# A fused attention and feed-forward layer: the first 16 V units reordered, and the loads that feed them

## The chip, the cores and the metric

The kernel runs on one Trainium2 chip, on 8 cores at once. Each core handles one sequence of 4096 tokens, with no exchange between cores. Times are device microseconds of the slowest core. The granted TensorE clock of a stretch is given as a share of full speed, which is 2.4 GHz.

## The reference, cut to what matters

```python
normed = (x - mu) * rsqrt(var + 1e-5) * norm_g + norm_b       # x: [4096, 1024] per core
hv = silu(normed @ W_h + b_h); v, gate = hv[..., :2048], hv[..., 2048:]
qk = silu(normed @ W_qk + b_qk)                               # 128 wide
quad_q, lin_q, quad_k, lin_k = heads of (qk * gamma + beta)
attn = square(relu(quad_q @ quad_k^T / 256 + bias))           # groups of 256 tokens
lin_kv = lin_k^T @ v / n                                      # sum over all 4096 tokens
out = gate * (attn @ v + lin_q @ lin_kv)
x = layernorm(x + (out @ W_o + b_o + x))
x = layernorm(x + relu(x @ W1 + b1) @ W2 + b2)
```

Since `lin_kv` sums over all tokens, V of all tokens is computed before the gate and the output can start.

## The kernel before, in words

The work has three stages: first V and qk for all tokens, then per block of 512 tokens the gate, the attention and W_o, and last the feed-forward part. The change concerns the start of the first stage.

The tokens stand in 32 tiles of 128, four to a block. Wv (the V half of W_h) has four slices of 512 columns. A **unit** is one tile by one slice: 8 matmuls of 128x512. There are 128 of them. `unit(u)` (line 39) gives tile and slice of unit u: the first 32 go through tiles 0 to 7 with slice 0, then with slice 1, 2 and 3. After them each tile takes its four slices in a row.

Every engine walks through u in a loop of its own. An engine executes its instructions strictly in the order written, so the slots below set the order.

- A tile t below 8 comes from DRAM in f32. VectorE makes its statistics (`stats_a`), GpSimd computes the scale from them, and writes the normalized tile in bf16 (`norm0`, lines 560 to 569). TensorE transposes it at slot `t_slot(t)` (8 short matmuls, line 680). ScalarE and VectorE each evict a part of it into `nfm` (lines 891 and 976); from tile 3 on ScalarE takes 5 and VectorE 3 of the 8 columns.
- A unit's PSUM result gets its bias from VectorE (`v_bias`, line 1013, which waits for that slice of the bias `bv`) and its silu from ScalarE (line 901). Both stand at slot `bias_slot(w)` (line 50). Before the change units 0 to 7 get them at slots 5 to 7.
- The products for qk (`qk`, line 691) of blocks 0 and 1 stand at units 10 and 14. GpSimd makes the four heads of it (`head_lk`, `heads`, lines 575 to 584); TensorE transposes lin_k (`lk_transpose`, line 698) at units 13 and 17.
- `linkv_unit` (line 724) adds V of a unit to `lin_kv`, one matmul each, starting at unit 16 (`linkv_at`).
- Tiles from 8 on pass through three f32 buffers and are transposed by DMA (`columns`, line 391).

Transfers: SyncE issues x, the first slice of Wv in four pieces (`wvf`, cast to bf16 by ScalarE at line 884, at slot 0), the bias slices, Wqk, and stores of V. These go to the hardware queue q1. GpSimd issues slices 1 to 3 of Wv as casting transfers, in two halves each (line 550), to the software queue q0: slice 1 after `norm0(3)`, slices 2 and 3 after `norm0(7)`. The second wait of SyncE is for `s_n0` 6, which means that tiles 0 to 5 are normalized. Then it loads x of tiles 8 to 10.

Until x and the weights have come, TensorE runs 20 warm matmuls and 8 more after each of the first two transposes (line 670).

Of the kernel before, what the change touches and what calls it, by code (L numbers as in the profile page):

```python
# [20 lines left out]
NT = 32  # L21
# [14 lines left out]

def unit(u):
    if u < 32:  # L40
        return u % 8, u // 8
    return u // 4, u % 4
# [6 lines left out]

def bias_slot(u):  # L50

    return (5, 5, 6, 6, 6, 7, 7, 7)[u] if u < 8 else u


def linkv_at(u):

    if u < 16:
        return ()
    if u < 24:
        return (2 * u - 32, 2 * u - 31)  # L60
    return (u - LAG,)


def t_slot(t):

    if t < 8:
        return (0, 0, 0, 1, 3, 4, 5, 6)[t]
    if t < 12:
        return (16, 19, 22, 25)[t - 8]
    return 16 * (t // 4) - 22 + 4 * (t % 4)  # L70


def stat_slot(t):

    return (9, 12, 18)[t - 8] if t < 11 else t_slot(t - 1)


def aff_slot(b):
# [2 lines left out]


def qk_slot(b):
    return (10, 14)[b] if b < 2 else 16 * b


def lkt_slot(b):
    return (13, 17)[b] if b < 2 else 16 * b + 4


def pieces_before(t):
# [15 lines left out]
def build_program():  # L107
# [145 lines left out]
    def v_buffer(w):  # L253

        if w < 16:
            return vse[:, w * 512:(w + 1) * 512]
        i = ((w // 4 - 4) % 3) * 4 + w % 4
        return vst[:, i * 512:(i + 1) * 512]

# [4 lines left out]
    def wt(eng, s, v):  # L264
        if v > 0:
            eng.wait_ge(S[s] if isinstance(s, str) else s, v)
# [33 lines left out]
    def rs_chain(gp, k):  # L300
        add_eps(gp, k)
        power(gp, k)
# [41 lines left out]
    def emit_sync(sy):  # L344
        def load_x_first(t):
            sy.dma_start(out=x_tile(t), in_=x_h[t * 128:(t + 1) * 128, :]).then_inc(d_xs[t], 16)

        def load_bv(s):
            sy.dma_start(out=bv[:, s * 512:(s + 1) * 512],
                         in_=bv_h[:, s * 512:(s + 1) * 512]).then_inc(d_bv[s], 16)  # L350
# [14 lines left out]
        load_wv_first(2)  # L365
        load_wv_first(3)
        load_x_first(4)
        load_x_first(5)
        load_x_first(6)
        load_bv(0)  # L370
        load_x_first(7)
        load_bv(1)
        sy.dma_start(out=wqkf[:], in_=wqk_h[:, :]).then_inc(d_wqk, 16)
        load_bv(2)
        load_bv(3)

        def load_x(t):
            i, n = ring(t - 8, 3)
# [12 lines left out]
            sy.dma_start_transpose(out=dst, in_=n0_tile(t)).then_inc(d_T[t % 2], 16)  # L391

        def store_v(q):
            wt(sy, "s_vsi", 4 * q + 4)
            if q < 4:
                src, landed = vse[:, q * 2048:(q + 1) * 2048], d_vse
            else:
                i = (q - 4) % 3
                src, landed = vst[:, i * 2048:(i + 1) * 2048], d_vst[i]
            if q < 8:  # L400
                s, t0 = q // 2, (q % 2) * 4
                dst = bass.AP(v_sp.tensor, t0 * 128 * HID + s * 512, [[HID, 128], [128 * HID, 4], [1, 512]])
            else:
                dst = v_sp[q, :, :]
            sy.dma_start(out=dst, in_=src).then_inc(landed, 16)
# [8 lines left out]
        load_x(8)  # L414
        load_x(9)
        load_x(10)
        for u in range(0, NU + 6):
            for t in range(8, NT):
                if t_slot(t) == u:
                    columns(t)  # L420
                    if t + 3 < NT:
                        load_x(t + 3)
            if u == 12:
                sy.dma_start(out=biasT[:], in_=rel_h[:, :]).then_inc(d_rel, 16)
            if u >= 5 and (u - 5) % 4 == 0 and (u - 5) // 4 < NT:
                store_v((u - 5) // 4)
            for b in range(NB):
                if qk_slot(b) + 3 == u and b < 6:
                    store_h(b)
            if u == 119:  # L430

                for i in range(2):
                    wt(sy, d_T[i], 16 * 12)
                for t in range(4):
                    q = tok_tile(t)
                    sy.wait_ge(*v_stored(q))
                    sy.dma_start(out=vb[:, t * 2048:(t + 1) * 2048], in_=v_sp[q, :, :]).then_inc(d_v[t], 16)
# [107 lines left out]
    def emit_gpsimd(gp):  # L545
        gp.memset(mhalf[:], -0.5).then_inc(S["s_initp"], 1)

        def load_wv(s):
            for c in (0, 2048):
                gp.dma_start(out=wv[:, s * 4096 + c:s * 4096 + c + 2048],  # L550
                             in_=wv_h[s - 1, :, c:c + 2048]).then_inc(d_wv[s], 16)

        wt(gp, "s_initp", 1)

        def norm0(t):
            j = t % 8
            if t != 7:
                rs_chain(gp, t)
            x_landed(gp, t)
            shift(gp, t)  # L560
            if t == 6:
                add_eps(gp, t + 1)
            wt(gp, "s_nm", t + 1)
            if t >= 10:
                wt(gp, d_T[t % 2], 16 * ((t - 8) // 2))
            gp.tensor_scalar(n0_tile(t), x_tile(t), rstd[:, j:j + 1], nmr[:, j:j + 1],  # L566
                             ALU.mult, ALU.add).then_inc(S["s_n0"], 1)
            if t == 6:
                power(gp, t + 1)

        def head_lk(b):
            wt(gp, "s_qks", b + 1)
# [18 lines left out]

        for t in range(NT):
            norm0(t)
            if t == 3:
                load_wv(1)
            if t == 7:
                load_wv(2)
                load_wv(3)
            if t in (8, 9):
                head_lk(t - 8)  # L600
                heads(t - 8)
            if t % 4 == 1 and t >= 13:
                head_lk(t // 4 - 1)
                heads(t // 4 - 1)

            for k in range(pieces_before(t), pieces_before(t + 1)):
                j, c = k // 4, (k % 4) * 1024
                gp.dma_start(out=wg[:, j * 4096 + c:j * 4096 + c + 1024],
                             in_=wg_h[j, :, c:c + 1024]).then_inc(d_wg[j], 16)
# [55 lines left out]
    def emit_tensor(te):  # L665
# [17 lines left out]
        def qk(b):  # L683
            wt(te, "s_wcq", 1)

            wt(te, "s_nfa", 8)
            wt(te, "s_nfd", 8)
            wt(te, "s_aff", b - 1)
            for c in range(8):
                o_ = b * 4096 + c * 512  # L690
                mm = te.matmul(pb[7][:], wqk[:, c * 128:(c + 1) * 128], nfm[:, o_:o_ + 512],  # L691
                               start=(c == 0), stop=(c == 7))
            mm.then_inc(S["s_qk"], 1)

        def lk_transpose(b):
            wt(te, "s_lk", b + 1)
            for i in range(4):
                mm = te.transpose(pT[:, i * 128:(i + 1) * 128], lkfm[:, i * 128:(i + 1) * 128], ident)
            mm.then_inc(S["s_lkT"], 1)
# [177 lines left out]
    def emit_scalar(sc):  # L877
# [25 lines left out]
        for u in range(NU):  # L903
            for t in tiles_at(u):
                nfm_evict(t)
                for c in ((0, 1), (2, 3, 4, 5, 6, 7))[t] if t < 2 else ():
                    cast_wv(c)
            if u == 8:
                sc.wait_ge(d_wqk, 16)
                sc.copy(wqk[:], wqkf[:]).then_inc(S["s_wcq"], 1)  # L910
            if (b := block_at(qk_slot, u)) is not None:
                wt(sc, "s_qk", b + 1)
                wt(sc, "s_hd", b)
                sc.activation(qkf[:], pb[7][:], AF.Silu, bias=prm[:, P_BQK:P_BQK + 1]).then_inc(S["s_qks"], 1)
            for w in range(u + 1):
                if bias_slot(w) == u:
                    v_silu(w)
# [43 lines left out]
    def emit_vector(ve):  # L961
# [7 lines left out]
        def stats_a(t):  # L969
            x_landed(ve, t)  # L970
            bn_stats(ve, x_tile(t), t)
# [48 lines left out]
        for u in range(NU):  # L1020
            for t in tiles_at(u):
                nfm_evict(t)
                if t < 3:
                    stats_a(t + 2)
            if 1 <= u < 4:
                stats_a(u + 4)
            for t in range(8, NT):
                if stat_slot(t) == u:
                    stats_a(t)
            for b in range(2, NB):  # L1030
                if u in (aff_slot(b), aff_slot(b) + 1):
                    affine(b, u - aff_slot(b))
            if u == 40:
                ve.wait_ge(d_rel, 16)
                ve.tensor_scalar(biasT[:], biasT[:], float(QKD) ** 0.5, None, ALU.mult).then_inc(S["s_init"], 1)
            if (b := block_at(lkt_slot, u)) is not None:
                wt(ve, "s_lkT", b + 1)
                if b >= 2:

                    wt(ve, "s_lkv", max(w for w in range(NU) if unit(w)[0] // 4 == b - 2) + 1)  # L1040
                ve.tensor_copy(lktm[:, (b % 2) * 512:(b % 2 + 1) * 512], pT[:, 0:512]).then_inc(S["s_lkt"], 1)
            if u in (123, 126):
                attn((u - 123) // 3)
            for w in range(u + 1):
                if bias_slot(w) == u:
                    v_bias(w)
# [168 lines left out]
```

## Time and profile before

| what | value |
|---|---|
| median of 3 runs | 1713.78 us (1713.61 to 1718.76) |
| the profiled execution, its own time | 1716.85 us |
| its span on the slowest core (core 6) | 1715.3 us |
| spans of the other cores | 1709.4 to 1712.6 us |
| PE matmul, busy | 1694.6 us (99%), 8164 instructions |
| DVE / ACT / POOL busy | 549.6 / 409.3 / 289.5 us |

The page gives, for each engine, its busy time, and cuts the span into 40 slices. PE shows 9 tenths or more in all slices but the first (7) and the last (8). PE is the matmul engine, DVE VectorE, ACT ScalarE, POOL GpSimd, SP SyncE. The profiled execution's own time stands 1.55 us above its span.

### The profile page before, as it was taken

How to read it: one execution, taken by the hardware profiler on the slowest of the kernel's cores; microseconds unless marked ns; L12 is line 12 of the kernel's file. 1: busy time of each engine (PE TensorE's matmuls, PEld its weight loads, DVE VectorE, ACT ScalarE, POOL GpSimd, SP SyncE). 2: the span in 40 equal slices, each digit the busy share in tenths (PEclk: the TensorE clock that was granted, in tenths of full speed). 3: DMA queues.
4: the chain of work that ended last, by engine and by line, in shares of the span. 5: the costliest groups of instructions: out<-in, count | busy, mean ns of one | idle time of the engine just before them, and what ended most of it. 6: DMA issues, size and time to landing. Idle time of an engine off the chain costs nothing.

```text
span 1715.3 us, 23484 instructions; the slowest of 8 cores (1709.4 to 1715.3 us)
## 1 busy us (share of the span) xinstructions
PE 1694.6 (99%) x8164; PEld 795.0 (46%) x8164; DVE 549.6 (32%) x927; ACT 409.3 (24%) x602; POOL 289.5 (17%) x459
## 2 busy tenths in 40 slices
PE   7999999999999999999999999999999999999998
PEld 3444444544544545545444444444444444444443
DVE  6465553445445455454102021030110201202102
ACT  5233333221221322222320402203113031140220
POOL 5444421042232231331200000000000000000000
PEclk9999999999999999999999999999999999999999
DMA  9996757745746647635941022101121011200101
GB/s 255 215 215 165 199 141 173 184 122 158 162 135 167 145 142 178 153 125 119 254 131 48 39 50 74 25 37 62 38 86 26 37 62 38 86 1 25 74 3 47
DMA packets 119153, 188.51 MB, mean 110 GB/s; under 512 B 64768, under 2 KB 68992, under 8 KB 119040
## 3 DMA queue, kind: packets, MB, share of 16 engines
q1 hardware_dynamic: 104352, 158.69, 29.2%
q0 software_dynamic: 14688, 28.32, 11.9%
q8 instruction: 70, 1.15, 0.3%
q14 instruction: 43, 0.35, 0.1%
HBM read 139.53 MB, written 69.47 MB: 122 GB/s over the span
## 4 chain that ended last, share of the span: by engine, by line
PE 96%; DMA 2%; POOL 0%; issue 0%; DVE 0%; SPq 0%; POOLq 0%; DVEq 0%
PE pb L872 26%; PE pb L849 26%; PE pb L815 13%; PE pb L781 13%; PE pb L715 12%; PE pb L803 3%; PE pb L724 2%; PE pb L797 2%; DMA xt<-x 1%; DMA xs<-x 1%; PE pb L691 1%; PE pb L739 0%; DVE bnst L272 0%; POOL n0s L566 0%; SPq L354 0%
## 5 line engine op out<-in xcount | busy, mean ns | idle before, releaser
L849 PE MATMUL pb<-xfm,w1s 128*128 128x512 bf16 x2048 | 443.3, 379 | 0.0
L957 ACT ACTIVATE h<-pb,prms 128x512 bf16<-128x512 f32 x256 | 176.1, 688 | 652.9 <-PE pb L849 652.9
L849 PEld LDWEIGHTS pb<-xfm,w1s 128*128 128x128 bf16 x2048 | 200.4, 98 | 241.6
L1114 DVE TENSOR_TENSOR xr<-pb,xr 128x512 f32<-128x512 f32 x64 | 44.3, 692 | 700.1 <-PE pb L872 700.1
L715 PE MATMUL pb<-wvs,nfm 128*128 128x512 bf16 x1024 | 242.2, 380 | 1.3 <-DVE vtmp L1013 0.6
L781 PE MATMUL pb<-nfm,wgs 128*128 128x512 bf16 x1024 | 240.6, 379 | 0.0
L872 PE MATMUL pb<-w2a,h 128*128 128x512 bf16 x1024 | 231.5, 379 | 0.0
L815 PE MATMUL pb<-wos,gated 128*128 128x512 bf16 x1024 | 224.6, 379 | 0.0
L293 POOL TENSOR_SCALAR veps<-mv 128x1 f32<-128x1 f32 x96 | 21.6, 225 | 1044.9 <-DVE mv L283 1043.7
L872 PEld LDWEIGHTS pb<-w2a,h 128*128 128x128 bf16 x1024 | 100.2, 98 | 120.8
L715 PEld LDWEIGHTS pb<-wvs,nfm 128*128 128x128 bf16 x1024 | 99.7, 98 | 119.6 <-issue 3.6
L815 PEld LDWEIGHTS pb<-wos,gated 128*128 128x128 bf16 x1024 | 100.2, 98 | 116.1
L781 PEld LDWEIGHTS pb<-nfm,wgs 128*128 128x128 bf16 x1024 | 100.2, 98 | 97.2
L1053 DVE TENSOR_TENSOR gated<-pb,gate 128x512 bf16<-128x512 f32 x128 | 88.4, 691 | 169.9 <-PE pb L803 118.0
L927 ACT ACTIVATE gate<-pb,prms 128x512 f32<-128x512 f32 x128 | 88.0, 687 | 206.5 <-PE pb L781 206.5
L1013 DVE TENSOR_TENSOR vtmp<-pb,bvs 128x512 f32<-128x512 f32 x128 | 87.7, 690 | 104.3 <-PE pb L715 103.1
L872 PE MATMUL pb<-w2b,h 128*128 128x512 bf16 x512 | 121.0, 379 | 0.0
L872 PE MATMUL pb<-w2c,h 128*128 128x512 bf16 x512 | 120.9, 379 | 0.0
L901 ACT ACTIVATE vst<-vtmp 128x512 bf16<-128x512 f32 x112 | 70.5, 630 | 154.0 <-DVE vtmp L1013 154.0
L272 DVE BATCH_NORM_STATS2 bnst<-xr 128x6 f32<-128x512 f32 x128 | 85.6, 690 | 17.2 <-DVE xr L1114 11.3
L658 POOL TENSOR_TENSOR xr<-xr,b2s 128x1024 f32<-128x1024 f32 x32 | 75.4, 2355 | 88.9 <-ACT xr L934 88.9
L934 ACT ACTIVATE xr<-xr,nmr,rstd 128x1024 f32<-128x1024 f32 x32 | 39.6, 1237 | 194.7 <-DVE x2bf L1079 194.7
(62 smaller groups left out, 896.0 us busy)
## 6 DMA issues: line engine op xcount, KB each, us to landing
vb<-v_sp SPq DMA_DIRECT2D x32, 512.0 KB, 6.2
xr<-x SPq DMA_DIRECT2D x32, 512.0 KB, 12.9
x_sp<-xr SPq DMA_DIRECT2D x32, 512.0 KB, 2.6
xr<-x_sp SPq DMA_DIRECT2D x32, 512.0 KB, 6.3
out<-xr SPq DMA_DIRECT2D x31, 512.0 KB, 2.6
v_sp<-vst SPq DMA_DIRECT2D x28, 512.0 KB, 5.7
xt<-x SPq DMA_DIRECT2D x24, 512.0 KB, 6.3
w_sp<-w POOLq DMA_DIRECT2D x32, 256.0 KB, 13.0
```

The source lines that it names most:

```text
L272: ve.bn_stats(bnst[:, c:c + 6], src[:, 512 * h:512 * h + 512]).then_inc(S["s_bn"], 1)
L658: gp.tensor_tensor(xr[:, i * 1024:(i + 1) * 1024], xr[:, i * 1024:(i + 1) * 1024], b2[:], ALU.add).then_inc(S["s_x2b"], 1)
L715: mm = te.matmul(pb[v_bank(u)][:], nfm_tok(t, c), wv[:, s * 4096 + c * 512:s * 4096 + (c + 1) * 512], start=(c == 0), stop=(c == 7))
L781: mm = te.matmul(pb[4 + n % 2][:], wg[:, w_:w_ + 128], nfm[:, o_:o_ + 512], start=(c == 0), stop=(c == 7))
L815: mm = te.matmul(pb[2 + h][:], gated[:, k * 512 + i * 128:k * 512 + (i + 1) * 128], wo[:, h * 8192 + k * 512:h * 8192 + (k + 1) * 512], st ...
L849: mm = te.matmul(pb[4 + n % 2][:], w1[:, w_:w_ + 128], xfm[:, x_:x_ + 512], start=(c == 0), stop=(c == 7))
L872: mm = te.matmul(ps[:], h1[:, ci * 512 + i * 128:ci * 512 + (i + 1) * 128], w_, start=(ci == 0), stop=(ci == 31))
L901: sc.activation(v_buffer(w), vtmp[:, (w % 3) * 512:(w % 3 + 1) * 512], AF.Silu).then_inc(S["s_vsi"], 1)
L927: sc.activation(gate[:, (n % 3) * 512:(n % 3 + 1) * 512], pb[4 + n % 2][:], AF.Silu, bias=prm[:, P_BG + e:P_BG + e + 1]).then_inc(S["s_gsi ...
L957: sc.activation(h1[:, ci * 512:(ci + 1) * 512], pb[4 + n % 2][:], AF.Relu, bias=prm[:, P_B1 + ci:P_B1 + ci + 1]).then_inc(S["s_h1"], 1)
L1013: ve.tensor_tensor(vtmp[:, (w % 3) * 512:(w % 3 + 1) * 512], pb[v_bank(w)][:], bv[:, s * 512:(s + 1) * 512], ALU.add).then_inc(S["s_vad"], 1)
L1053: ve.tensor_tensor(gated[:, e * 512:(e + 1) * 512], pb[n % 2][:], gate[:, (n % 3) * 512:(n % 3 + 1) * 512], ALU.mult).then_inc(S["s_gat"], 1)
```

## The change

It reorders the first 16 units by a table: four tiles by two slices, then tiles 4 to 7 by the same two slices. It follows this with other slots for transposes, statistics, bias and silu, qk, lin_k and `linkv`. SyncE loads only bias slice 0 behind x 4, then waits until tiles 0 to 3 are normalized, and only then loads bias slice 1, x 5 to 7 and Wqk; bias slices 2 and 3 come behind x 10. GpSimd issues the two halves of slice 1 after `norm0(1)` and `norm0(2)`, those of slice 2 after `norm0(5)` and `norm0(6)`, and slice 3 after the heads of both first blocks, which both now stand behind `norm0(9)`.

```diff
+FIRST = ((0, 0), (1, 0), (2, 0), (3, 0), (0, 1), (1, 1), (4, 0), (2, 1),
+         (3, 1), (4, 1), (5, 0), (5, 1), (6, 0), (6, 1), (7, 0), (7, 1))
 def unit(u):
+    if u < 16:
+        return FIRST[u]
...
 def bias_slot(u):
-    return (5, 5, 6, 6, 6, 7, 7, 7)[u] if u < 8 else u
+    return (0, 2, 2, 4, 5, 5)[u] if u < 6 else u
 def linkv_at(u):
-    if u < 16:
+    if u < 18:
         return ()
+    if u < 22:
+        return (3 * u - 54, 3 * u - 53, 3 * u - 52)
...
-        return (0, 0, 0, 1, 3, 4, 5, 6)[t]                 # t_slot
+        return (0, 0, 0, 2, 4, 8, 10, 12)[t]
-    return (9, 12, 18)[t - 8] if t < 11 else t_slot(t - 1)   # stat_slot
+    return (4, 6, 7, 9, 11, 18)[t - 5] if t < 11 else t_slot(t - 1)
-    return (10, 14)[b] if b < 2 else 16 * b                 # qk_slot
+    return (13, 14)[b] if b < 2 else 16 * b
-    return (13, 17)[b] if b < 2 else 16 * b + 4             # lkt_slot
+    return (15, 17)[b] if b < 2 else 16 * b + 4
...
         load_x_first(4)
+        load_bv(0)
+
+        wt(sy, "s_n0", 4)
+        load_bv(1)
         load_x_first(5)
         load_x_first(6)
-        load_bv(0)
         load_x_first(7)
-        load_bv(1)
         sy.dma_start(out=wqkf[:], in_=wqk_h[:, :]).then_inc(d_wqk, 16)
-        load_bv(2)
-        load_bv(3)
...
         load_x(10)
+        load_bv(2)
+        load_bv(3)
...
-            if t != 7:
-                rs_chain(gp, t)
+            rs_chain(gp, t)
...
-            if t == 3:
-                load_wv(1)
-            if t == 7:
-                load_wv(2)
-                load_wv(3)
-            if t in (8, 9):
-                head_lk(t - 8)
-                heads(t - 8)
+            if t in (1, 2, 5, 6):
+                load_wv(1 + t // 4, 1 - t % 2)
+            if t == 9:
+                for b in range(2):
+                    head_lk(b)
+                    heads(b)
+                for half in range(2):
+                    load_wv(3, half)
...
-            if 1 <= u < 4:
-                stats_a(u + 4)
-            for t in range(8, NT):
+            for t in range(5, NT):
                 if stat_slot(t) == u:
                     stats_a(t)
```

The four stores of early V follow the new order (at slots 5, 16, 10 and 17), `qk` also waits for the silu of the block before it, `lk_transpose` for the copy of the one before it, and the cast of Wqk moves from slot 8 to slot 10.

## Rows read from the trace of the kernel before

**Rows 1.** Cores: span and mean granted clock of three cores
```profile
core 1: 1712.6 us, clock 0.998
...
core 4: 1709.4 us, clock 1.000
...
core 6: 1715.3 us, clock 0.998
```

**Rows 2.** Line 691 (qk) to 70 us, core 1, then 4: first and last start
```profile
L691 PE MATMUL pb<-nfm,wqks x16: 379/379/379, 45.0 to 55.4; 128*128 128x512 bf16 x16
...
L691 PE MATMUL pb<-nfm,wqks x16: 379/379/379, 41.8 to 52.2; 128*128 128x512 bf16 x16
```

**Rows 3.** Chain that ended last, core 6: start us, us, what
```profile
63.63 0.43 PE pb L724 x2
64.06 0.22 PE pb L698 x4
64.28 1.73 PE pb L715 x8
```

**Rows 4.** Timeline, core 6, PE: start, us, line, out<-in, count, idle before
```profile
19.25 0.90 PE L715 MATMUL pb<-wvs,nfm 128*128 128x512 bf16 x2 [0.43 <-ACT wvs L884]
...
21.73 3.62 PE L715 MATMUL pb<-wvs,nfm 128*128 128x512 bf16 x16
...
52.92 0.38 PE L698 MATMUL pb<-prms,lkfm 128*128 128x128 bf16 x4 [3.76 <-POOL lkfm L575]
...
53.14 2.82 PE L715 MATMUL pb<-wvs,nfm 128*128 128x512 bf16 x8
```

**Rows 5.** Timeline, core 6, the other engines, 11 to 21 us
```profile
11.35 1.19 POOL L566 TENSOR_SCALAR n0s<-xs,rstd,nmr 128x1024 bf16<-128x1024 f32 x1 [0.18 <-POOL nmr L308]
...
18.49 1.14 ACT L884 CAST wvs<-wvf 128x512 bf16<-128x512 f32 x2 [0.19 <-DMA wvf<-wv]
...
19.89 1.31 POOL L550 DMA_DIRECT2D wvs<-wv  x2
20.18 1.29 DVE L272 BATCH_NORM_STATS2 bnst<-xs 128x6 f32<-128x512 f32 x2 [1.73 <-DMA xs<-x]
```

**Rows 6.** Instructions by line, core 6, 0 to 70 us: busy, mean ns
```profile
L891 ACT ACTIVATE nfm<-pb,prms 128x128 bf16<-128x128 bf16 x37 | 13.8, 458 | 13.6 <-PE pb L680 13.6
L1013 DVE TENSOR_TENSOR vtmp<-pb,bvs 128x512 f32<-128x512 f32 x19 | 12.5, 687 | 9.4 <-PE pb L715 9.4
L901 ACT ACTIVATE vse<-vtmp 128x512 bf16<-128x512 f32 x16 | 9.5, 632 | 15.5 <-DVE vtmp L1013 15.5
...
L582 POOL TENSOR_SCALAR hst<-qkf,gs,bs 128x512 bf16<-128x512 f32 x4 | 3.0, 772 | 0.0
```

**Rows 7.** DMA, hardware queue, core 6, 0-16.4, then 0-20: packets, MB, share
```profile
q1 hardware_dynamic: 1218, 4.02, 85.2%
...
q1 hardware_dynamic: 1572, 5.31, 87.8%
```

**Rows 8.** DMA, software queue, core 6, 23 to 24 us: its first packets
```profile
q0 software_dynamic: 5, 0.02, 11.2%
```

**Rows 9.** DMA, both queues, core 6, 26 to 34 us
```profile
q0 software_dynamic: 202, 0.76, 69.9%
q1 hardware_dynamic: 213, 0.55, 30.4%
```

**Rows 10.** DMA, both queues, core 6, 38 to 42 us
```profile
q0 software_dynamic: 135, 0.52, 75.0%
q1 hardware_dynamic: 125, 0.43, 32.1%
```

**Rows 11.** DMA issues, core 6: x of tile 4, issued at 5.70 us
```profile
xs<-x SPq DMA_DIRECT2D x1, 512.0 KB, 14.3
```

**Rows 12.** Tile wvs, core 6, 0 to 80 us: issue to landing
```profile
DMA to landing us min/median/max: 10.0/15.3/21.0
```

More of the change, by code:

```diff
@@ L255, in v_buffer @@
         if w < 16:
-            return vse[:, w * 512:(w + 1) * 512]
+            t, s = unit(w)
+            c = s * 8 + t
+            return vse[:, c * 512:(c + 1) * 512]
         i = ((w // 4 - 4) % 3) * 4 + w % 4
@@ L393, in store_v @@
         def store_v(q):
-            wt(sy, "s_vsi", 4 * q + 4)
+            wt(sy, "s_vsi", (4, 15, 9, 16)[q] if q < 4 else 4 * q + 4)
             if q < 4:
@@ L424, in emit_sync @@
                 sy.dma_start(out=biasT[:], in_=rel_h[:, :]).then_inc(d_rel, 16)
-            if u >= 5 and (u - 5) % 4 == 0 and (u - 5) // 4 < NT:
+            for q in range(4):
+                if u == (5, 16, 10, 17)[q]:
+                    store_v(q)
+            if u >= 21 and (u - 5) % 4 == 0 and (u - 5) // 4 < NT:
                 store_v((u - 5) // 4)
@@ L546, in emit_gpsimd, with load_wv @@
         gp.memset(mhalf[:], -0.5).then_inc(S["s_initp"], 1)
[L548 to L551, printed above, removed]
+        def load_wv(s, half):
+            c = half * 2048
+            gp.dma_start(out=wv[:, s * 4096 + c:s * 4096 + c + 2048],
+                         in_=wv_h[s - 1, :, c:c + 2048]).then_inc(d_wv[s], 16)
         wt(gp, "s_initp", 1)
@@ L556, in norm0 @@
             j = t % 8
-            if t != 7:
-                rs_chain(gp, t)
+            rs_chain(gp, t)
             x_landed(gp, t)
             shift(gp, t)
-            if t == 6:
-                add_eps(gp, t + 1)
             wt(gp, "s_nm", t + 1)
@@ L567, in norm0 @@
                              ALU.mult, ALU.add).then_inc(S["s_n0"], 1)
-            if t == 6:
-                power(gp, t + 1)
         def head_lk(b):
@@ L688, in qk @@
             wt(te, "s_aff", b - 1)
+            wt(te, "s_qks", b)
             for c in range(8):
@@ L696, in lk_transpose @@
             wt(te, "s_lk", b + 1)
+            wt(te, "s_lkt", b)
             for i in range(4):
@@ L907, in emit_scalar @@
                     cast_wv(c)
-            if u == 8:
+            if u == 10:
                 sc.wait_ge(d_wqk, 16)
```

## The prediction

> **What bounds the kernel now.** I read the cores first, then when each core comes to the dense part, then TensorE's own waits, and last the two DMA queues. The spans of cores 1, 4 and 6 are 1712.6, 1709.4 and 1715.3 us [rows 1]. The last matmul of qk for block 1 starts at 55.4 us on core 1 and 52.2 on core 4 [rows 2]; a matmul issues every 0.22 us and a unit takes 1.73 [rows 3], so with units 14 and 15 behind it unit 16 starts at 55.4 + 0.22 + 3.46 = 59.1 on core 1 and at 55.9 on core 4. On core 6 the first linkv products, which stand behind unit 16, start at 63.63 [rows 3], so unit 16 started at 61.9. The span less that start is 1653.5, 1653.5 and 1653.4 us. So from unit 16 to the end every core takes the same, nothing of the start is given back or lost later, and **the time is the start of unit 16 plus 1653.4 us**, as long as the dense part stays dense. The change acts on that one number.
>
> On core 6 the start holds one large wait of its own: 3.76 us of idle time before the lin_k transpose, which waited for GpSimd's lkfm, and behind it 8 matmuls in 2.82 us instead of 1.73, so at a lower clock [rows 3, 4]. GpSimd was itself behind x of tile 8. Without this wait and its 1.1 us core 6 would have started unit 16 at about 57, and core 1 would be the slowest, with 1712.6 + 1.55 us (what the profiled execution's own time stands above its span) = 1714.2. That is the median of the three runs within 0.4. So the profiled execution's 1716.85 has a mishap in it that the median does not, and my sum has to be held against 1713.78.
>
> **The change part by part.** It neither adds nor removes matmuls. It takes two units from each early tile instead of one, so that TensorE needs x more slowly, and it needs the second slice of Wv at unit 4 instead of unit 8. What it costs or gives is when unit 3 may start, and what holds units 3 to 15.
>
> *The transfers up to unit 3.* The first half of Wv's slice 1 is issued right behind the normalizing of tile 1, which ends at 11.35 + 1.19 = 12.5 us [rows 5]. GpSimd's 0.65 us per issue (half of the 1.31 for two, [rows 5]) fits in its idle time before tile 2, so it costs nothing there. Before, the issue at 19.89 [rows 5] had its first packets just before 24 us [rows 8], 3.9 us later. So slice 1 begins to move at 16.4 instead of 23.8 us. At 16.4 the hardware queue has moved 4.02 MB [rows 7]. In front of the end of x 4 stand five x tiles, four pieces of wvf (0.524 MB each) and prm (0.07): 4.79 MB; bias slice 0 makes it 5.05. Before, x 4 landed at 5.70 + 14.3 = 20.0 us [rows 11], when 5.31 MB had been moved [rows 7]: a transfer lands when some 0.52 MB more than its place in the queue has moved. Alone the queue moves (5.31 - 4.02) / 3.6 = 0.36 MB per us.
>
> With both queues busy the packets alternate: 125 hardware beside 135 software packets in one stretch, 213 beside 202 in the other [rows 9, 10]. Software moves 0.13 or 0.095 MB per us then, hardware 0.108 or 0.069 (smaller packets of the bias are in the second). Slice 1 has 1.05 MB, so it takes 8.1 to 11.0 us. I take 9.5, between the two, with 0.108 for hardware, since what stands in its queue here is x and wvf in full packets. At 25.9 us, then, slice 1 is through and hardware has moved 4.02 + 9.5 x 0.108 = 5.05 MB. The rest goes at 0.36: x 4 lands at 5.31 MB, 26.6 us; bias slice 0 at 5.57 MB, 27.4 us. The last piece of wvf (4.27 + 0.52 = 4.79 MB) lands at 16.4 + 7.1 = 23.5 us; before, ScalarE could cast it from 18.49 [rows 5].
>
> *The engines up to unit 3.* Unit 0 ends at about 25.0 instead of 20.15 [rows 4, 5], unit 1 at 26.7, the transposes of tile 3 at 27.2 (eight cost 0.44, twice the 0.22 for four of [rows 3]), unit 2 at 28.9. Unit 3 needs tile 3 in nfm. In front of that eviction VectorE now has the statistics of x 4 and the bias of unit 0, and ScalarE the silu of unit 0: at slot 0 instead of slot 5, and queued ahead of everything else on both engines. Statistics 26.6 to 28.1 (1.29 [rows 5] and the aggregate), bias 0.69 to 28.8, silu 0.63 to 29.5, five columns at 13.8 / 37 = 0.37 us [rows 6] to 31.4. Unit 3 starts at 31.5. TensorE stands for 2.6 us before it.
>
> *Units 3 to 15.* 13 units at 1.73, four sets of transposes at 0.44, two qk at 1.73 and the lin_k transpose at 0.22 are 28.0 us. In it x 5 to 7, issued behind the normalizing of tile 3, land by about 33; their statistics stand at slots 4, 6 and 7 and each leaves over 1 us until its transposes. The wait for lkfm goes: tile 9 is normalized at about 52 and qk of block 0 is done only after that, with over 3 us before the transpose needs it. One wait is new. The transposes of tile 7 stand at slot 12, two steps ahead of qk, which needs them evicted. Counted from the end of unit 11: bias and silu of unit 11 until 1.55 us (0.69 + 0.63 and the handovers), five columns until 3.4; TensorE is ready after 0.44 + 1.73 = 2.2 us. It waits 1.2 us. If VectorE's statistics of tile 9 at slot 11 come late, it is 2. The cast of Wqk (ScalarE, slot 10) lies in ScalarE's idle time, and the issues of slice 2 (two, 1.3 us of GpSimd) lie between tiles.
>
> Sum: 31.5 + 28.0 + 1.2 = 60.7 for the start of unit 16; plus 1653.4 is a span of 1714.1; plus 1.55 is **1715.7 us**. That is 1.2 below the profiled execution and 1.9 above the median. Bounds of the same case: slice 1 at the slow rates, 11 us and 0.069 MB per us, makes x 4 land at 28.9 and the sum 1718.0; a lower clock behind the wait of 2.6 us, at the price of core 6's, another 1.1; no wait for tile 7 and slice 1 in 8.1 us, 1713.
>
> **The rivals.** *Faster: the early slice does not hold up the hardware queue.* If hardware keeps its 0.36 MB per us until bias slice 0 is in, x 4 lands at 20.0 and bias slice 0 at 20.7. Then statistics to 21.7, bias 22.4, silu 23.1, evictions 25.0, unit 3 at 25.1, unit 16 at 54.3, and the time is 1654.95 + 54.3 = 1709.3; without the wait for tile 7 1708.1. For it: the first packets of a software transfer may come later than 3.9 us when GpSimd and VectorE are busy. Against it: in both stretches with two queues hardware fell to a third of its rate [rows 9, 10].
> The Trainium skill, "DMA: Bandwidth & Descriptors", section "Queues, rings and completion order", says that each DMA engine takes turns between the queues that have work, a whole packet at a time, and gives none of them precedence. The near-equal packet counts agree. By that rule the hardware queue cannot keep its rate beside slice 1, and the time is that of the sum and not 1709.3.
>
> *Slower: slice 3 of Wv comes too late for unit 24.* It is now issued behind the heads of block 1, and these wait for the lin_k transpose of block 0 at unit 15. From that transpose: lkfm of block 1 by 1.1 us, three heads at 0.77 [rows 6] by 3.4, issue, then 3.9 until data moves. Unit 24 is due 0.22 + 9 x 1.73 + 16 x 0.22 + 0.22 = 19.5 us from the transpose. Halves of a slice landed 10.0 to 21.0 us from their issue [rows 12]. At 0.13 MB per us the slice lands by 3.4 + 3.9 + 8.1 + 1.5 = 16.9: 2.6 us to spare, and 6 to spare at best. At 21 us the second half, issued 0.6 later, lands at 25, a wait of 5.5. It decides from 15.5 us between issue and landing on. Its price is up to 5.5 plus the 1.1 for the clock; at a wait of 4 the time is about 1720.5. For it: beside slice 3 now run the DMA transposes of tiles 9 and 10 and two stores of V. Against it: it is one slice, while 21.0 us was the last of four halves queued together.
>
> **How the numbers follow.** The forecast has 0.62, the faster rival 0.16, the slower 0.22. The forecast's own range is 1712 to 1719. The whole range reaches from 1708.5 to 1720.5, which leaves out the faster rival's lower half and the slower one's upper half. About 0.3% (5.1 us) is what a measurement of this kernel can tell from no change: faster is below 1708.6, and only the part of the faster rival that also loses the wait for tile 7 gets there, with cases I have not seen 0.12. Slower is above 1718.9: most of the slower rival and the upper edge of the forecast, 0.19. The rest, 0.69, is the same.
>
> **What would show it.** In the trace after: software packets from 16 or 17 us; the last wvf piece cast at about 23.5 instead of 18.5; bias of unit 0 on VectorE at 28, behind the statistics of x 4; TensorE waiting before unit 3 for ScalarE's eviction, 2 to 3 us; about 1 us before the first qk; none before the lin_k transpose; unit 16 at 60 to 61 on most cores; and from there 1653.4 to the end. If bias slice 0 is in by 22 us, or the span less the start of unit 16 is more than 1654, the forecast is wrong in its main step.

## The result and the profile after

The changed kernel is slower: 1728.7 us is the median of four runs (1727.0 to 1732.0), beside 1715.7 us for the kernel before. The ratio is 1.0079, with a 95% interval of 1.0066 to 1.0091. The forecast was 1715.7, its range ended at 1720.5. The kernel before stands higher than in the table of the prediction's time: three executions had a median of 1713.78 us, and with two more it is 1715.71. Executions in which half or all of the chip ran at a lower clock are left out of all times here.

The cores of the profiled execution come first, as in [rows 1]:

```profile
core 0: 1717.1 us, clock 0.998
core 1: 1728.0 us, clock 0.994
core 2: 1716.3 us, clock 0.998
core 3: 1723.4 us, clock 0.996
core 4: 1715.7 us, clock 0.998
core 5: 1726.4 us, clock 0.994
core 6: 1730.5 us, clock 0.993
core 7: 1718.3 us, clock 0.999
```

They fall into two groups. Cores 0, 2, 4 and 7 need 1715.7 to 1718.3 us, near the forecast span of 1714.1. Cores 1, 3, 5 and 6 need 5 to 15 us more. In the other three executions five, six and all eight cores end above 1720 us. The metric is the slowest core, so the question is what the second group suffers.

TensorE on core 6 (start us, us, line, count, idle before it and what ended it), where before only [rows 4] had a wait of this size:

```profile
17.07 1.46 PE L729 MATMUL pb<-wvs,nfm 128*128 128x512 bf16 x6
21.37 2.64 PE L729 MATMUL pb<-wvs,nfm 128*128 128x512 bf16 x10 [2.84 <-ACT wvs L898]
...
30.92 3.15 PE L729 MATMUL pb<-wvs,nfm 128*128 128x512 bf16 x7 [4.74 <-ACT nfm L905]
34.29 1.06 PE L692 MATMUL pb<-prms,n0s 128*128 128x128 bf16 x8 [0.22 <-issue]
35.14 7.84 PE L729 MATMUL pb<-wvs,nfm 128*128 128x512 bf16 x32
...
58.47 3.57 PE L704 MATMUL pb<-nfm,wqks 128*128 128x512 bf16 x8 [4.71 <-ACT nfm L905]
61.84 2.96 PE L729 MATMUL pb<-wvs,nfm 128*128 128x512 bf16 x8
...
99.42 3.57 PE L729 MATMUL pb<-wvs,nfm 128*128 128x512 bf16 x8 [3.65 <-DVE vtmp L1027]
```

Three waits are to be seen: 4.7 us before unit 3, 4.7 before the first qk, and 3.7 before unit 28, far behind the units that were reordered. Behind each, the eight matmuls take 3.4 us from start to start instead of 1.73 (one record is missing in the first). The granted clock of these stretches (31 to 34, 58.5 to 61.8 and 99.4 to 103 us) is 0.50, the level of 1.2 instead of 2.4 GHz; it is back at 1.00 about two units later. The first qk on core 0, of the other group:

```profile
53.25 1.89 PE L704 MATMUL pb<-nfm,wqks 128*128 128x512 bf16 x8 [1.91 <-ACT nfm L905]
```

VectorE on core 6, in the same form, shows what the waits go back to:

```profile
25.54 1.29 DVE L283 BATCH_NORM_STATS2 bnst<-xs 128x6 f32<-128x512 f32 x2 [7.10 <-DMA xs<-x]
...
27.51 0.69 DVE L1027 TENSOR_TENSOR vtmp<-pb,bvs 128x512 f32<-128x512 f32 x1 [0.37 <-issue]
...
53.44 1.29 DVE L283 BATCH_NORM_STATS2 bnst<-xt 128x6 f32<-128x512 f32 x2 [2.71 <-DMA xt<-x]
...
55.06 0.69 DVE L1027 TENSOR_TENSOR vtmp<-pb,bvs 128x512 f32<-128x512 f32 x1
...
96.95 1.29 DVE L283 BATCH_NORM_STATS2 bnst<-xt 128x6 f32<-128x512 f32 x2 [3.43 <-DMA xt<-x]
...
98.58 1.29 DVE L1027 TENSOR_TENSOR vtmp<-pb,bvs 128x512 f32<-128x512 f32 x2
```

Each time the statistics of a tile stand ahead of a unit's bias and wait for x. At 25.5 it is x 4, as forecast. At 53.4 it is x 9; the bias of unit 11 comes at 55.1, ScalarE's silu and its eviction of tile 7 behind that, and qk at 58.5:

```profile
55.85 0.63 ACT L915 ACTIVATE vse<-vtmp 128x512 bf16<-128x512 f32 x1 [3.37 <-DVE vtmp L1027]
56.38 1.84 ACT L905 ACTIVATE nfm<-pb,prms 128x128 bf16<-128x128 bf16 x5
```

Why x 9 is late, SyncE's queue shows (first the kernel before, then the changed one), and the hardware queue's share from 34 to 42 us (one packet):

```profile
27.98 1.90 SPq L381 DMA_DIRECT2D xt<-x  x3
```

```profile
21.74 0.43 SPq L386 DMA_DIRECT2D wqkf<-wqk  x1
41.15 1.29 SPq L392 DMA_DIRECT2D xt<-x  x3
```

```profile
q1 hardware_dynamic: 1, 0.00, 0.0%
```

SyncE waits for tile 5 to be normalized before it loads x 8 to 10. The statistics of tile 5 now stand at slot 4, behind units 1 to 3. So the DMA engines stand idle, and then x 8 to 10 start in the same moment as slice 2 of Wv (GpSimd issues it at 41.0).

On cores 0, 2, 4 and 7 x 8 to 10 and slice 2 are also issued together, and x 9 is in time. What differs is seen before slice 2 moves anything. The hardware queue of core 7 from 41.0 to 43.8 us, and of core 6 from 41.7 to 44.5, each from 0.6 us behind the issue of x 8:

```profile
q1 hardware_dynamic: 144, 0.52, 66.0%
...
q1 hardware_dynamic: 80, 0.33, 41.0%
```

Taking neighbours as pairs (0 and 1, 2 and 3, 4 and 5, 6 and 7), the late core is in each pair the one that issued x 8 later, here and in the profiled execution of experiment 4 too: eight pairs of eight. The first five packets of x 8 come 2.3 to 2.7 us behind the issue on the late core, 1.0 to 1.2 on the other. That neighbours get in each other's way would fit; no run tests it.

**Where core 6 loses its time, against the forecast.** Unit 16 starts at 70.0 us: it ends where the second lin_k transpose starts, 71.77, and takes 1.73. The forecast was 60.7. Unit 3 starts 0.6 earlier than forecast. Low clock on unit 3 and the transposes of tile 4 costs 2.0 (34.29 - 30.92 and 35.14 - 34.29, against 1.73 and 0.44), on units 4 to 7 0.8, a wait before the transposes of tile 6 0.6, qk 3.5 (4.7 instead of 1.2), low clock behind it 2.7. That is 9.6, less the 0.6 at unit 3 9.0 of the 9.3. From unit 16 to the end it is 1660.5 instead of 1653.5: the wait of 3.7 us, low clock 2.7, and 0.6 in small gaps. The cores of the good group start unit 16 at 60.7 to 63.0 and need 1654.6 to 1655.3 from there; each has one wait of 0.9 to 1.5 us near 88 us.

### The profile page after: what moved, and what is told of

It is laid out like the page before. It is cut to its first block, busy times and chain, and to the rows that moved or that the text cites. A ratio compares the mean times of both kernels' runs of the same rounds, so it can differ in the third digit from the quotient of the medians.

```text
span 1730.5 us, 23337 instructions; the slowest of 8 cores (1715.7 to 1730.5 us)
## 1 busy us (share of the span) xinstructions
PE 1692.0 (98%) x8002; PEld 796.8 (46%) x8164; DVE 549.5 (32%) x927; ACT 409.1 (24%) x602; POOL 290.0 (17%) x459
## 4 chain that ended last, share of the span: by engine, by line
PE 94%; DMA 2%; SPq 1%; issue 1%; DVE 1%; ACT 0%; POOL 0%; DVEq 0%; POOLq 0%; ACTq 0%
PE pb L886 25%; PE pb L863 25%; PE pb L829 13%; PE pb L795 13%; PE pb L729 11%; PE pb L817 3%; PE pb L811 2%; PE pb L738 1%; DMA xs<-x 1%; DMA xt<-x 1%; PE pb L704 1%; SPq L402 0%; SPq L392 0%; DVE bnst L283 0%; PE pb L753 0%
## 6 DMA issues: line engine op xcount, KB each, us to landing
xr<-x SPq DMA_DIRECT2D x32, 512.0 KB, 11.5
```

## The experiments

All ratios are to runs of the kernel before on the same chip. Lines of a diff begin with its change to the changed kernel, unless said otherwise.

**1. x 8 to 10 without the wait.**

```diff
-        wt(sy, "s_n0", 6)
         load_x(8)
```

> The changed kernel with one edit: the loads of x 8 to 10 are issued right behind Wqk, without the wait for tile 5 to be normalized. In the changed kernel the DMA engines stand idle from about 34 to 43 us, x 9 then lands beside slice 2 of Wv, VectorE's statistics of tile 9 wait for it, and the bias of unit 11, the silu and the eviction of tile 7 queue behind; qk waits 4.7 us on cores 1, 3, 5 and 6, and 1.9 on the others. Theory A (x 8 and 9 late): this wait falls to 1.2 to 1.9 us on all cores and with it the low clock behind it; the slowest core loses 3 + 2.5 us, and the time falls from 1729 to about 1721 to 1724. Theory B (the wait is ScalarE's own chain of silu and eviction, and the cores differ by something else): 1.9 and 4.7 us stay, and the time stays within 2 us of 1729.

Measured: ratio 1.0050 (1.0035 to 1.0065), 1724.3 us. The first qk waits 1.91 or 1.92 us on all eight cores, at full clock, and none of VectorE's statistics of tiles 8 and 9 waits for x. Theory A holds, its number at the upper edge (1721 to 1724). The slowest core is now 1723.3, the fastest 1717.5.

**2. The statistics of tile 9 one slot later.**

```diff
-    return (4, 6, 7, 9, 11, 18)[t - 5] if t < 11 else t_slot(t - 1)
+    return (4, 6, 7, 9, 12, 18)[t - 5] if t < 11 else t_slot(t - 1)
```

> The changed kernel with one edit: VectorE's statistics of tile 9 stand at slot 12 instead of 11, so behind the bias of unit 11 and the eviction of tile 7. The transfers stay as they are. Theory A (x 9 late, and harmful because it is queued ahead of the bias of unit 11): qk's wait falls to about 1.2 us on all cores, the same gain as issuing x 8 to 10 early, 1721 to 1724. Theory C (what costs is the clock or the contention of the transfers and not the place of the statistics): no change, about 1729. The bias of unit 12 may then wait for x 9, which TensorE would only feel later, at about unit 15.

Measured: 1.0050 (1.0035 to 1.0065), 1724.0 us. x 9 is as late as before (VectorE still waits up to 1.1 us for it), but qk waits 1.34 to 1.56 on all cores. The lateness of x 9 costs only because it is queued ahead of the bias of unit 11. With x 9 in time its statistics still cost 0.5 us there (1.91 against 1.41).

**3. Slice 3 of Wv ahead of the heads.**

```diff
+                for half in range(2):
+                    load_wv(3, half)
                 for b in range(2):
                     head_lk(b)
                     heads(b)
-                for half in range(2):
-                    load_wv(3, half)
```

> The changed kernel with one edit: slice 3 of Wv is issued directly behind the normalizing of tile 9, ahead of the heads of blocks 0 and 1, so about 10 to 14 us earlier. In the changed kernel TensorE waits before unit 28 for a bias on VectorE that stands behind the statistics of tiles 11 and 12 waiting for x, up to 3.7 us on core 6 with a low clock behind it, while slice 3 runs beside the DMA transposes. Theory D (slice 3 beside transposes and x 11 to 13 makes these late): the wait around 90 to 99 us goes and the span less the start of unit 16 falls from 1660 to 1654 on core 6; the time falls by 3 to 6 us to 1723 to 1726. Theory E (these x are late because their own issue is late, whatever runs beside): the wait stays, time within 2 us of 1729.

Measured: 1.0102 (1.0086 to 1.0119), 1733.0 us, not faster than the changed kernel, whose interval it overlaps. Both theories missed. On core 1 TensorE waits 7.9 us at 97 us and VectorE 8.6 us for x. Slice 3 is issued there at 54.2 us instead of 71.2, 2 us behind the DMA transpose of tile 8, which landed 27.4 us after its issue. The next transpose held SyncE's queue for 9.1 us, from 77.3 us on, when slice 3 had just landed (about 77.3), so slice 3 didn't run beside it. The steps between were not followed.

**4. Bias and silu of unit 0 later.**

```diff
-    return (0, 2, 2, 4, 5, 5)[u] if u < 6 else u
+    return (2, 2, 2, 4, 5, 5)[u] if u < 6 else u
```

> The changed kernel with one edit: bias and silu of unit 0 stand at slot 2 instead of slot 0, so behind the eviction of tile 3. The statistics of tile 4 keep their place ahead of it. Forecast by the prediction's step: tile 3's eviction no longer waits for bias slice 0, only VectorE's part for the statistics of x 4 (to 27.1 us); unit 3 starts at about 28 instead of 30.9 to 32, the wait before it falls from 2.7 to 4.7 us to 1 to 2, the time falls by about 3 us to 1726. If later waits (x 9, bound by tile 5's statistics at slot 4) take it back, the gain is under 1 us.

Measured: 1725.9 and 1724.9 us, two runs, too few for an interval. The forecast for it was about 1726. Core 1, unit 3, as it starts now (30.9 to 32.3 in the changed kernel):

```profile
28.44 1.89 PE L729 MATMUL pb<-wvs,nfm 128*128 128x512 bf16 x8 [2.06 <-DVE nfm L990]
```

On seven cores unit 3 starts at 27.8 to 29.6 us, 2.5 us earlier in the mean, and the cores of the good group (here 1, 3, 5 and 6) come to 1714.0 to 1715.8. The others still have 4.9 to 5.3 us before qk and end at 1723.6 to 1724.4. What was forecast for this step is right.

**5. Slice 3 right behind slice 2**, with the edit of experiment 1.

```diff
-            if t in (1, 2, 5, 6):
-                load_wv(1 + t // 4, 1 - t % 2)
+            if t in (1, 2):
+                load_wv(1, 1 - t % 2)
+            if t in (5, 6):
+                for half in range(2):
+                    load_wv(t - 3, half)
...
-                for half in range(2):
-                    load_wv(3, half)
```

> The changed kernel with the loads of x 8 to 10 not waiting (as in the first experiment), and slice 3 of Wv issued right behind slice 2 (slice 2 after tile 5, slice 3 after tile 6), so that no slice of Wv runs beside the DMA transposes of tiles 9 to 12. In the first experiment these transposes took 3.2 to 6.2 us of SyncE's queue beside slice 3, x 12 and 13 came late behind them, and TensorE waited about 1 and 1.5 to 2.2 us near 85 and 92 us. Theory F (4 KB packets of slice 3 alternate one to one with the short packets of the transposes and starve them): both late waits go on all cores, the span less the start of unit 16 is back at 1653.5, and the time falls from 1724.3 to about 1720.5. Rival G (x 12 and 13 are late because the new order shifts their issue): both waits stay and the time is within 1 us of 1724.3.

Measured: 1.0023 (1.0013 to 1.0033), 1719.5 us. Theory F holds. SyncE's queue on core 1 in experiment 1, then here (DMA transposes and the load between them):

```profile
66.79 3.21 SPq L402 DMA_TRANSPOSE nfm<-n  x1
70.09 6.22 SPq L392 DMA_DIRECT2D xt<-x  x1
76.40 2.08 SPq L417 DMA_DIRECT2D v_sp<-vst  x1
78.58 6.03 SPq L402 DMA_TRANSPOSE nfm<-n  x1
```

```profile
67.19 3.70 SPq L402 DMA_TRANSPOSE nfm<-n  x1
70.98 1.73 SPq L392 DMA_DIRECT2D xt<-x  x1
...
74.52 4.00 SPq L402 DMA_TRANSPOSE nfm<-n  x1
...
82.28 1.22 SPq L402 DMA_TRANSPOSE nfm<-n  x1
```

And the two DMA queues of core 1 from 78 to 82 us (packets, MB, share), in the same order:

```profile
q0 software_dynamic: 237, 0.51, 92.5%
q1 hardware_dynamic: 233, 0.08, 11.8%
```

```profile
q1 hardware_dynamic: 1047, 0.68, 91.6%
q0 software_dynamic: 128, 0.23, 30.8%
```

Packet by packet the queues alternate, 237 to 233, but the hardware ones are short: 0.08 MB in 4 us. The transposes at 67 and 74.5 us still hold SyncE's queue for 3.7 and 4.0 us here, though the software queue has only 46 packets from 72 to 78 us, so slice 3 isn't the whole of their time. No core waits for a late x behind unit 16 any more, and the first linkv on core 1 starts at 69.48, so unit 16 at 69.48 - 5.40 = 64.1 (its distance to the first linkv is that of core 6 above), and 1717.7 - 64.1 is 1653.6 again; the other cores give 1653.5 to 1653.7.

**6. The repairs together.** Experiments 1, 2 and 4, and slices 2 and 3 behind tiles 4 and 5.

```diff
-            if t in (1, 2, 5, 6):
-                load_wv(1 + t // 4, 1 - t % 2)
+            if t in (1, 2):
+                load_wv(1, 1 - t % 2)
+            if t in (4, 5):
+                for half in range(2):
+                    load_wv(t - 2, half)
...
```

> The changed kernel with all repairs: x 8 to 10 without the wait, bias and silu of unit 0 at slot 2, statistics of tile 9 at slot 12, slices 2 and 3 of Wv issued behind tiles 4 and 5. If the causes add up: unit 3 at 28 to 29 us, qk waits 1.3 to 1.4 us, no wait behind unit 16; 1720.5 less 3 (unit 3) less 0.5 (statistics of tile 9) is about 1717, with less low clock 1715 to 1716, so level with the kernel before. If the order of units itself costs more than these waits, it stays at 1720 or above.

Measured: 1.0014 (1.0004 to 1.0024), 1718.0 us. Unit 3 starts at 26.9 to 30.4. x 8 is late again on six cores (VectorE waits 0.9 to 4.1 us), since the slices start a tile earlier; TensorE waits up to 3.6 us on core 2 for the eviction behind it.

**7. And the statistics of tile 4 out of the way.** To experiment 6 this is added:

```diff
-        return (0, 0, 0, 2, 4, 8, 10, 12)[t]
+        return (0, 0, 0, 2, 5, 8, 10, 12)[t]
...
-    return (4, 6, 7, 9, 12, 18)[t - 5] if t < 11 else t_slot(t - 1)
+    return (2, 5, 6, 7, 9, 12, 18)[t - 4] if t < 11 else t_slot(t - 1)
...
-                if t < 3:
+                if t < 2:
                     stats_a(t + 2)
-            for t in range(5, NT):
+            for t in range(4, NT):
```

> As the repaired kernel, and also: statistics of tile 4 behind the eviction of tile 3 (slot 2 instead of 0), transposes of tile 4 at slot 5 instead of 4, statistics of tile 5 at slot 5. VectorE's part of tile 3 then waits neither for x 4 nor for the bias. Expected: unit 3 at about 26 instead of 28 to 29, and 1.5 to 2.5 us less time, 1712.5 to 1714.5, below the kernel before. If the wait moves on to tile 4 (its transposes waiting for GpSimd's normalizing), the gain is under 1 us.

Measured: 1.0018 (1.0009 to 1.0027), 1718.3 us: a miss. The wait before unit 3 is 0.5 us, but unit 3 starts at 28.0 to 30.2. Unit 0 waits 2.1 to 3.9 us for the last casts, and units 0 and 1 run at a low clock. The bound is now the last piece of wvf beside slice 1, as experiment 10 shows by moving slice 1.

**8. The kernel before, x 8 to 10 without the wait** (the same lines, in the kernel before).

> The kernel before with one edit: x 8 to 10 are loaded directly behind the last bias slice, without the wait for tile 5. It removes what core 6 suffered in the profiled execution (x 8 landing at 47.3 us beside slices 2 and 3 of Wv, 3.76 us of wait before the lin_k transpose and the low clock behind it). If that mishap is what makes some executions of the kernel before 1716 to 1719, the spread goes and the median is 1713 to 1714; x 8 to 10 may delay nothing needed earlier, since they stand last in the queue. If slices 1's packets are held up by them, units 8 and later wait for slice 1 and the time rises by 1 to 2 us.

Measured: 1.0003 (0.9992 to 1.0013), 1715.7 us, 1713.5 to 1717.1: no difference to be told, where 1713 to 1714 was forecast. On core 7 of the profiled execution x 8 was issued at 17 us, VectorE still waited for it until 49.3, and the lin_k transpose waited 4.75 us. So the wait for tile 5 was not the only reason for that mishap. What is left of it stays open.

**9. Slice 1 one tile later.**

```diff
-            if t in (1, 2, 5, 6):
-                load_wv(1 + t // 4, 1 - t % 2)
+            if t in (2, 3, 5, 6):
+                load_wv(1 + t // 4, t - 2 if t < 4 else 1 - t % 2)
```

> The changed kernel with one edit: the halves of slice 1 are issued behind tiles 2 and 3 instead of 1 and 2, some 3.7 us later. The prediction's first term says that slice 1 beside the last piece of wvf, x 4 and bias slice 0 moves these from 18.4, 20.0 and 21 to 20 to 23.5, 26.6 and 27.4 us. By it: unit 0 no longer waits for the cast (2.2 to 4 us in the changed kernel) and no low clock follows; x 4 and bias slice 0 land 1 to 3 us earlier, unit 3 starts 1 to 3 us earlier; unit 4 needs the whole slice 1 and may wait for it until 30 or 31 us. Alone, with the late waits still there, the time falls by 1 to 3 us from 1729. If the time does not move, slice 1's arrival at unit 4 has taken the place of the wait.

Measured: 1.0036 (1.0022 to 1.0050), 1722.8 us; 1 to 3 us less were forecast, and it is 6 less. The other faults are still in it, but x 9 is late on two cores only (by 1.6 and 1.3 us), where qk waits 3.6 and 3.3 us, so part of the gain is there. VectorE has x 4 at 20.2 to 21.3 us instead of 24.4 to 26.9, and unit 3 starts at 25.6 to 26.7. But unit 4 now waits, here on core 4:

```profile
31.83 8.75 PE L729 MATMUL pb<-wvs,nfm 128*128 128x512 bf16 x32 [3.48 <-DMA wvs<-wv]
```

**10. All repairs, and slice 1 one tile later** (experiments 7 and 9 together).

> The repaired kernel of the seventh experiment with slice 1 issued behind tiles 2 and 3. There unit 0 still waits 2.1 to 3.9 us for the last casts, with 10 matmuls in 4.2 us instead of 2.6 behind it. Expected: unit 0 ends at 20 to 21 on all cores, unit 3 starts at 25 to 26 instead of 28 to 30, unit 4 waits 0 to 2 us for slice 1; 2 to 4 us less than the seventh, a ratio of 0.998 to 1.000 to the kernel before. If it stays at 1.0018, slice 1 is the bound at unit 4 and the order four tiles by two slices can't win.

Measured: 1.0028 (1.0015 to 1.0040), 1721.8 us, no better than experiment 7 (the intervals overlap); 2 to 4 us less were forecast. Core 0, unit 3 and unit 4:

```profile
24.25 1.89 PE L729 MATMUL pb<-wvs,nfm 128*128 128x512 bf16 x8 [0.48 <-ACT nfm L905]
30.07 3.57 PE L729 MATMUL pb<-wvs,nfm 128*128 128x512 bf16 x8 [3.94 <-DMA wvs<-wv]
```

Unit 3 is 4 us earlier than in the seventh, and all of it goes into the wait for slice 1 (2.9 to 4.3 us) and the low clock behind it.

**11. The kernel before with slice 1 early**, the one part alone.

```diff
-            if t == 3:
-                load_wv(1)
+            if t in (1, 2):
+                load_wv_half(1, t - 1)
```

> The kernel before with one part of the change alone: the halves of slice 1 are issued behind tiles 1 and 2 instead of both behind tile 3. The old order needs slice 1 only at unit 8, and x one tile per unit. By the prediction's first term the last wvf piece lands up to 4 us later and x 4 at 26 to 27 instead of 20; unit 3 needs it through statistics, GpSimd and transposes about 5 us later than before. Units 0 to 7 move by 4 to 6 us, and with the low clock 5 to 7 us are added: 1720 to 1722. If the hardware queue keeps its rate beside slice 1, nothing changes (within 1 us).

Measured: 1.0015 (1.0001 to 1.0029), 1719.3 us. The mechanism is as expected: x 4 comes at 25.0 to 28.8 us instead of 20.2 on core 6 [rows 5], and the last casts hold unit 0 for 1.3 to 3.5 us. Of the time only 2.6 us are lost, half of the forecast, but the cores lose more: seven of them end 2.9 to 5.7 us later than in the profiled execution before (1714.9 to 1718.3 us instead of 1709.4 to 1712.6). Core 6 ends 0.6 earlier, since the 3.76 us before the lin_k transpose [rows 4] are gone there. So part of the price is hidden in the time: it goes by the slowest core, and that one had a mishap before which this execution doesn't have.

**12. The repairs, with the slices where experiment 5 had them** (experiments 2, 4 and 5 together).

> The changed kernel with x 8 to 10 without the wait and slices 2 and 3 of Wv behind tiles 5 and 6 (the fifth experiment), and bias and silu of unit 0 at slot 2, statistics of tile 9 at slot 12. The sixth experiment had the slices behind tiles 4 and 5, and there x 8 came late beside them on five cores (1.1 to 4.1 us on VectorE, up to 3.6 us on TensorE). If the causes add up: no wait for x 8 on any core, and 1719.5 less 3 (unit 3) less 0.5 (tile 9) is 1716, a ratio of 0.999 to 1.001 to the kernel before. If it is 1.0014 again, the gain at unit 3 is taken back by the low clock of units 0 and 1, which no repair so far touches.

Measured: 1.0016 (1.0005 to 1.0028), 1719.5 us, 1714.8 to 1721.1. The time is that of experiment 5; 1716 was forecast. In the profiled execution the cores end at 1712.1 to 1713.8 except two, which lose 3 and 5 us at a place of their own. Core 0, at 158 us, where the tiles pass one by one and VectorE had stood 3.9 us for a DMA transpose:

```profile
158.50 2.36 PE L729 MATMUL pb<-wvs,nfm 128*128 128x512 bf16 x8 [3.64 <-DVE vtmp L1027]
```

The causes add up on the typical core (27.0 to 30.0 for unit 3, 1.41 before qk, the median span of the cores 3.9 us shorter than in experiment 5), but in five of nine runs some core ends at 1718.0 to 1719.6. That such a wait is behind it is seen in the profiled one alone, and why it comes was not tested. No version beats the kernel before.

## Why the prediction was wrong, step by step

- **The time is the start of unit 16 plus 1653.4 us.** Right as arithmetic (1653.6 in experiment 5), wrong as a guard. It holds "as long as the dense part stays dense", and the changed kernel lost 7.0 us of core 6 there, and 1.1 to 1.8 on the cores of the good group.
- **The transfers up to unit 3.** Right. Forecast: x 4 at 26.6, bias slice 0 at 27.4. Measured on core 6: x 4 issued at 5.70 landed 19.8 us later, at 25.5, and the bias came on VectorE at 27.5. The two queues from 18 to 20 us moved 0.22 and 0.20 MB with 54 and 52 packets, as in [rows 10]. The last wvf piece was cast at 20.6 (20.0 to 22.4 on the cores), not 23.5: this term was up to 3 us too large. The first software packets came at 17.0, when the hardware queue stood at 4.28 MB, and the piece had landed at 4.68 MB instead of 4.79; in between the queue moved 0.11 MB per us, as forecast. Experiment 11 shows the contention by itself, experiment 9 its removal.
- **Unit 3 at 31.5, behind x 4, bias 0 and silu 0.** Right: 30.0 to 32.3 on the cores, and experiment 4 took 2.5 us of it away. The wait was 4.7 us on core 6 instead of 2.6, because unit 2 ended earlier than forecast; 1.8 to 3.1 us on the others.
- **The low clock behind that wait.** Left out of the sum, and 1.1 us in the bounds; it cost 2.8 on core 6 (2.0 and 0.8 above), and 2.7 behind each of the two later waits.
- **One new wait, 1.2 us before qk.** Its own chain was well sized: 1.41 in experiment 2. The statistics of tile 9 ahead of it add 0.5 even when x 9 is there. If they came late, the prediction gave the wait 2 us; it was 4.7 to 4.9.
- **The step that failed: "x 5 to 7 land by about 33; their statistics stand at slots 4, 6 and 7".** The sum stopped there. It never asked when SyncE passes its second wait, which hangs on tile 5's statistics, now behind units 1 to 3. Before, that wait ended at 28 to 30 us; now it ends at 38 to 41, with the DMA engines idle from 34 on core 6. x 9 has no time to spare any more, and is late on four of eight cores: 4.7 to 4.9 us before qk instead of 1.9, and the low clock. Experiments 1 and 2 each remove it, from different ends, with the same 4.4 to 4.7 us. That the late issue costs this is shown by experiment 1. Why four cores are late and four are not stays open; the sharing with slice 2 alone can't be it, since all eight have it.
- **The slower rival.** It named the right cause (slice 3 now runs beside the transposes) and the wrong victim. Slice 3 reached unit 24 in time on every core of the changed kernel (unit 24 waited 0.3 and 0.8 us on one core each in experiments 1 and 2). It was the transposes that starved and, behind them in SyncE's queue, x 11 to 13, in front of whose statistics VectorE then stood. Experiment 5 removes this for another 4.8 us. With the two mishaps gone the kernel is at 1719.5, 0.23% above the kernel before and within the first range; what is left of it lies before unit 4, where experiments 4, 7, 9, 10 and 11 look.
- **The faster rival** was excluded for the right reason. Experiment 10 adds why its time can't be had: with the hardware queue free, slice 1 comes 3 to 4 us after unit 3 has ended.

The Trainium skill, "DMA: Bandwidth & Descriptors", section "Queues, rings and completion order", has the engines take turns packet by packet. I used it for bytes of equal packets. Experiment 1 agrees with it and shows the side that decided here: 237 packets against 233, and six times the bytes.

## What to carry to other kernels

When a step moves, follow each wait of the queues behind it to what releases it, even where no data of the moved step is involved: here a guard in SyncE's program cost 4.4 us of 13. A wait for a transfer belongs behind the instructions that the busy engine needs next, not ahead of them. Large transfers in one queue and short-packet transposes in another should not overlap: here they shared by packets and not by bytes.

## What the runs showed of the hardware

- A wait of TensorE can cost more than itself: behind the 4.7 us before qk, qk and the next unit took 3.37 and 2.80 us (from start to start) instead of 1.73 each. This is 2.7 us more, at 1.2 GHz. It isn't so behind every wait: on core 2 unit 3 waited 3.07 us and then took 1.73. There the low clock (granted 0.57 from 22 to 26 us) stood behind the wait for the last cast, two units earlier.
- Neighbouring cores are not alike. On the core of a pair that issued x 8 later, the first packets of the hardware queue came 2.3 to 2.7 us behind the issue instead of 1.0 to 1.2, and those of slice 2 3.9 to 4.3 us instead of 2.7 to 3.0, in all eight pairs looked at. The time of the issue alone doesn't tell: core 3 issued at 39.95 us and was late, core 7 at 40.42 and was not. In the changed kernel x 9 landed 7.0 to 8.1 us behind its issue on one core of a pair, 11.5 to 11.9 on the other.
- A DMA transpose held SyncE's queue 1.2 us with the software queue empty (experiment 5, 82.3 us), and 6.0 us beside slice 3 (experiment 1, 78.6 us). The 9.1 us of experiment 3 were not beside slice 3.
